# Two edits to an attention loop: one VectorE instruction in place of four, and a product issued half a step earlier

## The reference

```
attn = softmax(q @ k.T / sqrt(HD))
mod  = attn * coh;  mod = mod / (mod.sum(-1) + 1e-8)
out  = ((1 - fi) * mod + fi * fa) @ v
```

## Time and profile before

| | us |
|---|---|
| median of 3 runs | 544.99 |
| lowest and highest of them | 536.79 and 546.53 |
| the profiled execution | 536.53 |
| its span in the trace | 534.7 |
| TensorE busy | 471.4 |
| VectorE busy | 315.3 |
| ScalarE busy | 277.0 |

### The profile page before, as it was taken

The page is one execution under the profiler, slowest core; times in us unless marked ns, Lnnn a source line. Parts: engine busy times, 40 slices in busy tenths (PEclk is TensorE's granted clock), DMA queues, the critical chain, the costliest instruction groups (busy, mean ns, idle before and its releaser), DMA issues.

```text
span 534.7 us, 8218 instructions
## 1 busy us (share of the span) xinstructions
PE 471.4 (88%) x2872; PEld 308.5 (58%) x2872; DVE 315.3 (59%) x863; ACT 277.0 (52%) x496; POOL 115.6 (22%) x141
## 2 busy tenths in 40 slices
PE   6758999879879999999999988989999988889970
PEld 6757989743334334335987873334434333779970
DVE  5543876476868878852353667877887761402223
ACT  4353465574546666774636544556566663116540
POOL 6460005005154111100100000101111015422551
PEclk9988999996989999988999987999999999889995
DMA  8935102009910000200000000000000005330004
GB/s 314 392 109 154 31 26 64 26 16 215 410 69 2 0 2 1 78 2 1 0 1 0 2 1 1 1 0 2 0 1 1 0 2 190 159 105 5 19 17 122
DMA packets 22567, 33.99 MB, mean 64 GB/s; under 512 B 2349, under 2 KB 18344, under 8 KB 21760
## 3 DMA queue, kind: packets, MB, share of 16 engines
q1 hardware_dynamic: 20192, 28.46, 15.9%
q0 software_dynamic: 2336, 5.02, 3.0%
HBM read 24.91 MB, written 9.85 MB: 65 GB/s over the span
## 4 chain that ended last, share of the span: by engine, by line
issue 66%; PE 22%; DVE 3%; ACT 3%; SPq 2%; DMA 2%; another core or an unknown queue 1%; DVEq 0%; POOLq 0%; POOL 0%; ACTq 0%
PE PS L678 5%; PE PS L809 3%; PE PS L818 3%; PE PS L669 3%; PE PS L686 2%; PE PS L407 2%; SPq L1581 1%; PE PS L647 1%; ACT Kp L935 1%; DVE x_tok L1531 1%; DMA early<-early_dram 1%; DMA wb<-packed_rows 1%; DVE c L1210 1%; DMA xT_yT<-result_pairs 1%
## 5 line engine op out<-in xcount | busy, mean ns | idle before, releaser
L1351 DVE TENSOR_REDUCE mx<-PS 128x1 f32<-128x512 f32 x256 | 164.8, 686 | 49.8 <-PE PS L506 49.2
L951 ACT ACTIVATE wc_late<-PS 128x1024 f32<-128x1024 f32 x128 | 123.8, 1022 | 59.2 <-PE PS L524 56.2
L506 PE MATMUL PS<-Kp,Qs 128*128 128x512 f32 x256 | 107.9, 481 | 14.2 <-DVE mx L1351 7.8
L506 PEld LDWEIGHTS PS<-Kp,Qs 128*128 128x128 f32 x256 | 44.1, 195 | 92.5 <-DVE mx L1351 50.0
L539 PE MATMUL PS<-wc_late,v_c 128*16 128x512 f32 x512 | 70.3, 622 | 1.2 <-issue 1.2
L1647 POOL CAST Kp<-Ks 32x512 fp32r<-32x512 f32 x40 | 24.4, 610 | 122.4 <-ACT Ks L930 120.5
L524 PE MATMUL PS<-Qm,Kp 32*128 32x512 f32 x256 | 36.3, 520 | 2.5 <-ACT wc_late L951 1.4
L1066 ACT ACTIVATE work<-PS,late 128x160 f32<-128x160 f32 x64 | 20.0, 398 | 34.1 <-PE PS L809 33.0
L1260 DVE SCALAR_TENSOR_TENSOR x_tok<-PS,cw,x_tok 128x128 f32<-128x128 f32 x64 | 18.0, 344 | 32.3 <-PE PS L778 32.3
L778 PEld LDWEIGHTS PS<-wb,work 128*128 128x128 f32 x256 | 32.2, 198 | 1.7 <-issue 0.5
L778 PE MATMUL PS<-wb,work 128*128 128x128 f32 x256 | 32.6, 282 | 0.0
(11 more groups left out here) (278 smaller groups left out, 729.8 us busy)
## 6 DMA issues: line engine op xcount, KB each, us to landing
wa<-wa_dram SPq DMA_DIRECT2D x8, 514.0 KB, 8.6
wa<-wc_dram SPq DMA_DIRECT2D x2, 2048.0 KB, 17.6
wc_late<-wc_dram SPq DMA_DIRECT2D x2, 2048.0 KB, 10.6
sel<-sel_dram POOLq DMA_DIRECT2D x2, 1024.0 KB, 5.8
wb<-wb_dram SPq DMA_DIRECT2D x1, 2048.0 KB, 16.6
y_pairs<-work SPq DMA_DIRECT2D x28, 64.0 KB
late<-late_dram SPq DMA_DIRECT2D x1, 1508.0 KB
packed_rows<-ao SPq DMA_DIRECT2D x1, 1290.0 KB
```

The lines of the kernel that those rows point to most:

```text
L506: filled(mm(p, Qs[:, G % 3, qt * P:(qt + 1) * P], Kp[:, G % 3, j, :], start=True, stop=True), (L, "max", G, qt, j))
L951: A(E4[:, 2 * (i % 2) + jp, :, :], p, ACT.Exp, scale=float(HD[L]) ** -0.5).then_inc(taken[f"s{jp}"], 1)
L1351: V.reduce_max(mx[:, G % 2, qt, j:j + 1], p, AX.X).then_inc(taken[filled_at[key][0]], 1)
```

## The change

`norm` writes its result with one instruction over all 4 blocks of queries in place of one for each block. The job `maxT` of group `G + 1` is done in step `kt` = 2 at place 1, as the first job there, in place of step `kt` = 3 at place 0; in group 0 it stays where it was. Since both engines follow `jobs`, TensorE's product and VectorE's sum both move. In steps 6 and 22 of `L` = 0 and 6, 10, 14, 22 and 26 of `L` = 1 it now stands ahead of the step's own job.

```
@@ -299,7 +299,7 @@
             if place == 0:
                 return {0: [("stackK2", G + 2)] * (more and G > 0), 1: [("stackQ", G + 2)] * more,
                         2: [("turn", G - 1)] * (G > 0),
-                        3: [("maxT", G + 1)] * (G + 1 < NGB)}[kt]
+                        3: [("maxT", G + 1)] * (G == 0)}[kt]
...
-            return out + [("stackK", G + 3)] * (kt == TPB - 1 and G + 3 < NGB)
+            return ([("maxT", G + 1)] * (kt == TPB - 2 and 0 < G < NGB - 1) + out
+                    + [("stackK", G + 3)] * (kt == TPB - 1 and G + 3 < NGB))
...
                     a = ao[:, :, :].rearrange("p t (h d) -> p t h d", d=hd)
-                    for t in range(TPB):
-                        last = V.tensor_tensor(a[:, t, g * HPG:(g + 1) * HPG, :], o[:, t, :, 0:hd], wide(rden[:, t, :], hd),
-                                               ALU.mult)
-                    last.then_inc(taken["mi"], 1)
+                    V.tensor_tensor(a[:, :, g * HPG:(g + 1) * HPG, :], o[:, :, :, 0:hd],
+                                    rden[:, :, :].unsqueeze(3).to_broadcast([P, TPB, HPG, hd]), ALU.mult).then_inc(taken["mi"], 1)
```

## The result

The changed kernel is slower: 547.47 us in the median of 6 runs (542.72 to 555.1), against 537.92 us for the kernel before in its 6 (536.22 to 546.53). The ratio is 1.0164, with a 95% interval from 1.0105 to 1.0223: slower, and whether by more than 2% stays open. The profiled execution took 542.72 us with a span of 540.7 us, against 536.53 and 534.7: 6.0 us more span.

What follows compares the result with a forecast made beforehand. TensorE's program order was taken as near the bound. Six spots +8.1, clock +1.0, plain groups -0.8, step 26 -0.7 and last norm -0.3 gave +7.3 us, added to the median 544.99: 552.3 us, range 541 to 558.

Steps and rivals of the forecast that it cites:

- What bounds the kernel: TensorE's program order bounds the span; in a plain group the move can take away only a pair's 0.46 us wait.
- `maxT` in step 26: Both attentions, no maxima left: Qm comes ahead of the logits chain, 0.35 us gained in each, -0.7 us.
- The norm: One instruction of 0.28 us for four of 0.48: 0.20 saved; 0.3 us counted for the norm after the last group.
- `maxT` in a plain group: Four groups without a job in step 2: 0.2 us left of the 0.46 us stall, -0.8 us in all.
- `maxT` ahead of another job: Six spots: the job behind maxT waits for the shared slot until Qm is written; 1.1 to 1.5 each, 8.1 us.
- The clock: Behind the new pauses of 1.3 to 1.5 us the granted clock falls once, at about 1.0 us: +1.0.
- The rival of falls in most spots: Clock falls in most of the six spots, slower than 2%: five falls, sum 11.3 us, up to 556 to 558; chance 0.17.
- The rule of the Trainium skill: Rival: only pauses some times longer than the new ones lower the clock; sum 6.3 us, 551.3; no fall at all 0.15.
- The even exchange, not slower: Rival: maxT and the job merely change places, the six spots cost 0; sum -1.8 us, 543.2 us; chance 0.10.

Runs made afterwards that it cites:

- e1: Kernel before with the wide norm instruction alone, maxT left where it was: ratio 0.9922 to the kernel before.
- e7: Changed kernel with five unread products filling TensorE's pause behind maxT in step 10 of the second attention only: one run, 530.55 us (before on that chip: 525.64).
- e4: Changed kernel with maxT moved only in the six groups whose step 2 has a job of its own: ratio 1.0184 to the kernel before.
- e2: Changed kernel with the four narrow norm instructions back, so the move of maxT alone: ratio 1.0281 to the kernel before.
- e5: Changed kernel with the step's own job ahead of maxT in step 2 of a group: ratio 1.0122 to the kernel before.
- e9: Changed kernel with maxT in step 2 at place 1 and the step's own job in step 3 at place 0, groups 1 to 5: ratio 0.9994 to before.
- e8: Changed kernel with five unread products in the pauses of all six spots where a job follows maxT: ratio 1.0133 to the kernel before.
- e6: Changed kernel with maxT ahead of the place-1 pair of maxima, on TensorE and VectorE: ratio 1.0199 to the kernel before.

## Why the prediction was right

Direction, size and the deciding mechanism were right: +7.3 us forecast, +6.0 in span and a ratio of 1.0164, which is some 8.8 us. That the span lies so near the forecast is in part luck: the terms below come to more, and a low clock in the trace of before hid some of it. The median of 547.47 lies 4.8 below the 552.3 that I gave, because I added the sum to a median of three runs of before, 544.99, which six runs put at 537.92; the range, 541 to 558, had room for that. Point by point:

- **What bounds the kernel: right in the plain groups,** not in the last ones (`maxT` in step 26, below). The 0.46 us of a pair's wait was all that the move could take, and `Qm` was not waited for in a plain group.
- **The norm: right.** 291 ns for the 0.28 us taken in the second attention, 0.19 to 0.21 us saved in the five groups of the second attention that have a job (e1), and 0.15 lost in the plain one. The saving at the end of the last norm was not measured by itself.
- **`maxT` in a plain group: right,** 0.32 us each in the first attention and 0.11 in the second for the 0.2 of the forecast; the handed-on wait is in the trace (0.88 us for the pair at 193.51). The place-0 pair kept more of its wait than I said, 0.89 us for the 0.75 foretold. From scores 12 to scores 16 it took 14.13 us for 14.47 before.
- **`maxT` ahead of another job: right, and the term that decided.** A pause of 1.36 us ahead of `coh`; its group longer by 12.11 - 10.68 = 1.4 us at the full clock (e7), as forecast (the terms written there, 1.81 less 0.49, add up to 1.3). `qk` of the second attention 0.94 for 1.1, `vsum` 1.29, `proj` 1.65 and 1.39 for 1.3 to 1.5. Only `qk` of the first attention was larger, 2.60 for 1.4: its step lies in a stretch of low clock in every trace, which I had left out of that term. e4 and e2, with as short a low stretch as before, show 1.9; against e1, with as long a one as after, it is 1.2. What the prediction takes from Part 1 of the page of the Trainium skill "TensorE: Matmul & The Clock Gate" stands there for the weight loads; that the matmuls keep program order stands in its Part 2.
- **`maxT` in step 26: wrong in sign.** I forecast 0.35 us of gain in each attention, by following `Qm` to the scores of step 28; it cost 0.8 in the first and 0.1 in the second (0.3 against e4). The waits for `Qm` did go. What I missed is that without maxima ScalarE's exponentials set the pace there. ScalarE in steps 26 and 27 of the first attention before, then steps 26 to 28 after:

```profile
228.72 3.95 ACT L951 ACTIVATE wc_late<-PS 128x1024 f32<-128x1024 f32 x4 [1.41 <-PE PS L524]
```

```profile
234.00 0.63 PE L514 MATMUL PS<-ident_r,MP 128*128 128x128 f32 x4 [0.17 <-DVE ao L1377]
234.56 0.51 PE L525 MATMUL PS<-Qm,Kp 32*128 32x512 f32 x4
...
235.16 3.77 ACT L952 ACTIVATE wc_late<-PS 128x1024 f32<-128x1024 f32 x4 [0.87 <-PE PS L525]
...
237.15 0.50 PE L525 MATMUL PS<-Qm,Kp 32*128 32x512 f32 x2 [0.33 <-ACT wc_late L952]
```

  `maxT` waits for the norm and the scores of step 27 wait behind it, so ScalarE stands still for 0.87 us in the middle of exponentials that ran back to back before, and step 28 waits for it in turn: 7.80 us for 7.00, also against e1. The first attention's row shows it in every kernel that moves `maxT` there.
- **The clock: right in kind, a half too small in price.** One fall in a spot, behind `coh`, 1.5 us for the 1.0 taken, and in all three traces with that pause. The rival of falls in most spots did not come: at the other pauses of 1.3 to 1.5 us the clock stayed at 1.00 in after. One reading was off: I put the new pauses between the 0.98 us up to 435.38 and the pause of 321.00, but that one lasts 1.23 us and is the shorter, as the timeline of before shows:

```profile
322.32 0.49 PE L506 MATMUL PS<-Kp,Qs 128*128 128x512 f32 x1 [1.23 <-DVE mx L1351]
```

  So the rows spoke more for the rival of many falls than I allowed, and that exactly one spot had a fall is in part luck. The rule of the Trainium skill, page "TensorE: Matmul & The Clock Gate", section "Why this matters for your kernels", which advises against pauses of over some 3 us, does not clear these: 1.17 us (e2), 1.35 (e4) and 1.36 (after) came ahead of a fall here, and 0.48 us in e5, next to products with few columns.
- **The even exchange, not slower:** did not happen (e4); as a real exchange, with half a step between the two, it does (e9).

The terms as measured come to +10.6 us (9.2 by way of e1); that the span grew by only 6.0 is mostly due to the low clock at the end of the first attention in the trace of before (3.9 us). Against the forecast of 7.3 the change itself had 1.6 us more from step 26 and 0.5 from the clock.

## What to carry to other kernels

When a step is moved in a hand-ordered program, look first at who claims the same buffer next: two users back to back cost the whole round trip through the reader's queue, here 1.4 us at the full clock, and with a block of scores and a pair between them 0.2 to 0.3 us on average were left (e9). Ask in every stretch anew which engine sets the pace, since the same move gained 0.3 us where TensorE and VectorE alternated and lost 0.8 us where ScalarE ran without pause. And set steps of the same kind side by side from the traces: effects of 0.3 us stood out clearly there, while whole runs of one kernel lay 10 us apart.

## What the runs showed of the hardware that I had not expected

A pause of TensorE of 1.17 to 1.36 us followed by eight products of 16 columns stood ahead of a granted clock of 0.50 in three traces of three (e2, e4, after), at a price of 1.5 us, and five unread products of 512 columns in the pause prevented it in both kernels that had them (e7, e8). In the one trace of e5 a pause of 0.48 us behind the same small products had a fall behind it as well, while 0.35 us ahead of them in e6 and 0.19 in e9 had none.

Small products are not always part of it: in e5 the clock also fell behind pauses of 1.72 and 1.73 us between products of 512 and of 128 columns (`qk`, then `maxT`), where after, with 1.26 and 1.45 us between the same two in the other order, kept 1.00. What tells the cases apart is not shown by these runs.

One VectorE instruction over three free dimensions, with 128 elements a partition, PSUM and a broadcast input, took 291 ns where a plain one of that size took 280.
